# Feed-forward norm weights applied to the turned rows, and a local output projection in four steps

## The reference

```python
x = x + o @ wo                       # local output projection
h = shift_token(x)
mu = h.mean(-1, keepdims=True)
var = h.var(-1, keepdims=True)
h = (h - mu) / jnp.sqrt(var + 1e-05) * lg + lb
h = h @ w1 + b1
a, g = jnp.split(h, 2, axis=-1)
h = a * jax.nn.gelu(g, approximate=False)
x = x + h @ w2 + b2
```

## Time and profile before

| what | value |
|---|---|
| median of 3 runs | 1886.77 us (1885.72 to 1888.03) |
| the profiled execution: its own time | 1886.66 us |
| its span on the core | 1885.10 us |
| time outside the span | 1.56 us |
| TensorE busy share of the span | 93% |
| mean granted TensorE clock | 0.949 of full speed |

### The profile page before, as it was taken

How to read it: one execution, slowest core, us unless ns; L and a number is a source line. 1 busy time by engine, 2 the same in 40 slices (tenths; PEclk the granted TensorE clock), 3 DMA queues, 4 the chain that set the end, 5 groups by cost and what they waited for, 6 DMA issues and landing times. The chain is left out here.

```text
span 1885.1 us, 42756 instructions
## 1 busy us (share of the span) xinstructions
PE 1759.3 (93%) x14072; PEld 1335.8 (71%) x14072; DVE 1144.2 (61%) x2863; ACT 982.9 (52%) x1897; POOL 864.0 (46%) x886
## 2 busy tenths in 40 slices
PE   5899999999779999999988999699999999989997
PEld 3566656666357777777777888577777777768886
DVE  5567766677566766766633433777666776435554
ACT  2556566565545655555553444455565655444443
POOL 3333333333426665555633333555555665235544
PEclk7899888998889999999989999899999999999999
DMA  4433343333010101010023222101100000212221
GB/s 142 143 123 98 123 130 116 123 115 108 26 56 2 33 33 33 33 33 22 11 69 101 67 66 69 56 12 34 33 33 10 24 33 22 80 56 79 89 88 46
DMA packets 105656, 121.29 MB, mean 64 GB/s; under 512 B 23386, under 2 KB 78340, under 8 KB 105604
## 3 DMA queue, kind: packets, MB, share of 16 engines
q1 hardware_dynamic: 99412, 98.08, 16.7%
q0 software_dynamic: 6192, 22.55, 3.3%
HBM read 82.55 MB, written 37.77 MB: 64 GB/s over the span
## 5 line engine op out<-in xcount | busy, mean ns | idle before, releaser
L485 DVE TENSOR_REDUCE a_negm<-d 128x2 f32<-128x256 f32 (+3 forms) x256 | 201.1, 815 | 122.2 <-PE d L631 120.3
L448 ACT ACTIVATE a_PT<-b 128x384 f32<-128x384 f32 (+1 forms) x384 | 185.0, 524 | 135.6 <-PE b L670 69.7
L901 POOL TENSOR_TENSOR l_t<-l_t,l_t 128x512 f32<-128x512 f32 x128 | 165.4, 1293 | 148.3 <-DVE l_t L1053 147.3
L1071 DVE CUSTOM_DVE_ANT_0 d<-d,window 128x256 f32<-128x256 f32 (+1 forms) x512 | 184.3, 421 | 29.1 <-PE d L1171 29.0
L985 ACT ACTIVATE l_PT<-b 128x512 f32<-128x512 f32 (+1 forms) x256 | 125.4, 542 | 109.8 <-PE b L1213 106.3
L1479 POOL TENSOR_TENSOR m_hid_lo<-m_hid,m_hid_hi 128x512 fp32r<-128x512 f32 x80 | 105.1, 1323 | 154.7 <-ACT m_hid_hi L1537 154.5
L1099 PE MATMUL d<-w,l_xt 128*128 128x512 f32 x384 | 165.9, 432 | 3.2 <-DVE l_t L1053 2.3
L1100 PE MATMUL d<-w,l_xt 128*128 128x512 f32 x384 | 152.4, 397 | 0.0
L1101 PE MATMUL d<-w,l_xt 128*128 128x512 f32 x384 | 151.7, 395 | 0.0
L1205 PE MATMUL b<-l_Q,l_K 64*128 64x256 f32 x1536 | 140.3, 295 | 3.2 <-ACT l_PT L985 3.2
L919 POOL TENSOR_TENSOR l_zl<-l_zt,l_zh 128x512 fp32r<-128x512 f32 x64 | 85.7, 1348 | 120.4 <-ACT l_zh L991 120.4
(11 more groups left out here) (228 smaller groups left out, 4915.3 us busy)
## 6 DMA issues: line engine op xcount, KB each, us to landing
a_Q<-qk_parts SPq DMA_DIRECT2D x192, 64.0 KB, 2.1
a_K<-qk_parts SPq DMA_DIRECT2D x192, 64.0 KB, 2.1
qk_parts<-a_qk_hi SPq DMA_DIRECT2D x32, 256.0 KB, 2.1
qk_parts<-a_qk_lo SPq DMA_DIRECT2D x32, 256.0 KB, 2.1
xin<-after_attn SPq DMA_DIRECT2D x32, 256.0 KB, 3.0
m_xr<-after_attn SPq DMA_DIRECT2D x16, 512.0 KB, 3.9
after_attn<-rows_out POOLq DMA_DIRECT2D x14, 512.0 KB, 5.3
xin<-in_L_attn_x SPq DMA_DIRECT2D x8, 512.0 KB, 3.3
```

The costliest lines, as they stand in the source:

```text
L448: nc.scalar.activation(PT[:, p // PG % 2, 2 * (p % PG) + hh, QOFF[t]:QOFF[t] + nq], SC[hh][:, 0:nq], ACT.Exp, scale=AD ** -0.5).then_inc(e ...
L485: dve.tensor_reduce(negm[:, q, 2 * p:2 * p + 2], MX[i % 2][:, :, 0:nk], AX.X, ALU.max, negate=True).then_inc(max_done, 1)
L901: pool.tensor_tensor(t1[:, par, w, :], t1[:, par, w, :], t2[:, par, w, :], ALU.add)\
L1071: m = dve.tensor_tensor_reduce(out=o, in0=o, in1=mask, scale=-1.0, scalar=-NEG, op0=ALU.add, op1=ALU.min, accum_out=negm[:, q + t, p // 2, ...
```

## The change

Four things are different.

The opening of the first stage gets a list of its own (`OPENING`) instead of the filtered list `FIRST` plus `nw:0`. The two lists hold the same steps in the same order.

The local `out` step becomes four steps `out:0` to `out:3`, one for each 128 rows. They stand one behind the other wherever `out:0` stood, so no instruction changes its place. One wait moves: PE's wait on `mrow_done` (ACT's copy of the turned maxima out of the bank that rows 1 and 3 use) stood before all of it and stands now before `out:1`.

The norm weight leaves the split of `w1`: both halves of the tails are now split by one instruction each, and the low parts are plain subtractions. `gam` is loaded with the small vectors.

In `f_te`, ACT now does four instructions instead of two: for each half it reads the turned rows from PSUM twice with `scale=gam` and `bias=bet`, once into `ht_hi` and once into a float32 tile `hf`, which takes the place of `hn` in memory. DVE subtracts `hf` and `ht_hi`, both in SBUF, where it read PSUM before. ACT waits for both halves to be turned, and for the first batch for the small loads. Step `w` is gone, with its wait on `bias_done` ahead of `f_w1`.

```diff
@@ local attention, tensor @@
             elif name == "out":
-                pe.wait_ge(zl_done, b * PAIRS + PAIRS)
-                pe.wait_ge(own.lo_done, KT + 1)
-
-                pe.wait_ge(mrow_done, b * 2 + (2 if isinstance(b, int) else 3))
-                for t in range(TB):
-                    pe.wait_ge(y_done, b * TB + max(t - 1, 0))
...
+                if i == 0:
+                    pe.wait_ge(zl_done, b * PAIRS + PAIRS)
+                    pe.wait_ge(own.lo_done, KT + 1)
+                elif i == 1:
+                    pe.wait_ge(mrow_done, b * 2 + (2 if isinstance(b, int) else 3))
+                pe.wait_ge(y_done, b * TB + max(i - 1, 0))
...
@@ feed-forward weights @@
-            act.wait_ge(self.w_loaded, 32)
-            copy(self.w_hi[:, n, :], self.w_raw[:, n, :], ACT.Copy, scale=gam[:, n:n + 1]).then_inc(self.hi_done, 1)
+            act.wait_ge(self.w_loaded, 16)
+            copy(self.w_hi[:, n, :], self.w_raw[:, n, :], ACT.Copy).then_inc(self.hi_done, 1)
...
-            dve.scalar_tensor_tensor(out=self.w_lo[:, n, :], in0=self.w_raw[:, n, :], scalar=gam[:, n:n + 1],
-                                     in1=self.w_hi[:, n, :], op0=ALU.mult, op1=ALU.subtract).then_inc(self.lo_done, 1)
+            dve.tensor_tensor(self.w_lo[:, n, :], self.w_raw[:, n, :], self.w_hi[:, n, :], ALU.subtract)\
+                .then_inc(self.lo_done, 1)
@@ feed-forward, scalar @@
             if name == "f_m":
                 act.wait_ge(rstd_done, 4 * b + 4)
                 if not isinstance(b, int):
-                    act.wait_ge(turned, b * KT)
+                    act.wait_ge(lo_done, b * KT)
...
             elif name == "f_te":
+                if isinstance(b, int):
+                    act.wait_ge(own.loaded, 96)
+                else:
+                    act.wait_ge(w1_done, b * NT)
+                act.wait_ge(turned, b * KT + KT)
                 for k in range(KT):
-                    act.wait_ge(turned, b * KT + k + 1)
-                    if k == 0 and not isinstance(b, int):
-                        act.wait_ge(w1_done, b * NT)
-                    nc.scalar.activation(ht_hi[:, k, :], FB[k][:, :], ACT.Identity).then_inc(hi_done, 1)
+                    nc.scalar.activation(ht_hi[:, k, :], FB[k][:, :], ACT.Identity, scale=gam[:, k:k + 1],
+                                         bias=bet[:, k:k + 1])
+                    nc.scalar.activation(hf[:, k, :], FB[k][:, :], ACT.Identity, scale=gam[:, k:k + 1],
+                                         bias=bet[:, k:k + 1]).then_inc(scaled, 1)
@@ feed-forward, vector @@
-            if name == "w":
-                dve.wait_ge(bias_full, lay + 1)
...
             elif name == "f_te":
                 for k in range(KT):
-                    dve.wait_ge(hi_done, b * KT + k + 1)
-                    dve.tensor_tensor(ht_lo[:, k, :], FB[k][:, :], ht_hi[:, k, :], ALU.subtract)\
+                    dve.wait_ge(scaled, b * KT + k + 1)
+                    dve.tensor_tensor(ht_lo[:, k, :], hf[:, k, :], ht_hi[:, k, :], ALU.subtract)\
@@ feed-forward, tensor @@
-            elif name == "w":
-                pe.wait_ge(*before.maxima)
-                pe.wait_ge(own.mix_set, 2)
-                pe.wait_ge(own.loaded, 80)
-                for c in range(2 * NF + 1):
...
                 if name == "f_w1" and isinstance(b, int):
-                    if i == 0:
-                        pe.wait_ge(bias_done, 2 * lay + 2)
-                    else:
-                        pe.wait_ge(*before.scores)
+                    pe.wait_ge(*(before.maxima if i == 0 else before.scores))
@@ the joins from local attention to feed-forward @@
-        +f_te:0 pv:1 st:5 ps:2 sv:1 z:1 nm:0 +w:0 st:6 zn:1 zs:0 ns:0 pv:2 sv:2 zs:1 z:2 st:7 zn:2 pv:3 ps:3 +set:0 sv:3
-        zs:2 ns:1 z:3 zn:3 zs:3 +f_w1:0 +f_w1:1 ns:2 out:0 +f_h:0 +f_h:1 +banks:0 +nw:0"""),
+        +f_te:0 pv:1 st:5 ps:2 sv:1 z:1 nm:0 st:6 zn:1 zs:0 ns:0 pv:2 sv:2 zs:1 z:2 st:7 zn:2 pv:3 ps:3 +set:0 sv:3
+        zs:2 ns:1 z:3 zn:3 zs:3 +f_w1:0 +f_w1:1 ns:2 out:0 out:1 out:2 out:3 +f_h:0 +f_h:1 +banks:0 +nw:0"""),
```

More of the change, by code:

```diff
@@ L874, in do @@
                 ahead.load_h(sp, 0)
-            elif name == "out" and isinstance(b, int):
+            elif name == "out" and i == TB - 1 and isinstance(b, int):
                 sp.wait_ge(y_done, end * TB)
@@ L919, in do @@
                 pool.tensor_tensor(zl[:, i, :], zt[:, i, :], zh[:, i, :], ALU.subtract).then_inc(zl_done, 1)
-            elif name == "out" and not isinstance(b, int):
+            elif name == "out" and i == TB - 1 and not isinstance(b, int):
                 pool.wait_ge(y_done, b * TB + TB)
@@ L1336, in high @@
     def high(self, act, n):
-        copy, gam = self.nc.scalar.activation, self.gam
+        copy = self.nc.scalar.activation
         if n < KT:
-            act.wait_ge(self.w_loaded, 32)
-            copy(self.w_hi[:, n, :], self.w_raw[:, n, :], ACT.Copy, scale=gam[:, n:n + 1]).then_inc(self.hi_done, 1)
+            act.wait_ge(self.w_loaded, 16)
+            copy(self.w_hi[:, n, :], self.w_raw[:, n, :], ACT.Copy).then_inc(self.hi_done, 1)
         else:
             act.wait_ge(self.mix_set, 2)
-            for k in range(KT):
-                copy(self.mix_hi[:, k, :], self.mix_raw[:, k, :], ACT.Copy, scale=gam[:, k:k + 1])\
-                    .then_inc(self.hi_done, 1)
+            copy(self.mix_hi[:, :, :], self.mix_raw[:, :, :], ACT.Copy).then_inc(self.hi_done, 1)
             act.wait_ge(self.w2_loaded, 64)
@@ L1379, in feed_forward @@
     NF, TAIL, AT, MIX, NT = own.NF, own.TAIL, own.AT, own.MIX, own.NT
-    w_raw, mix_raw, b1, bet, h, h_in = own.w_raw, own.mix_raw, own.b1, own.bet, own.h, own.h_in
+    b1, gam, bet, h, h_in = own.b1, own.gam, own.bet, own.h, own.h_in
     w_hi, w_lo, mix_hi, mix_lo, w2_hi, w2_lo = own.w_hi, own.w_lo, own.mix_hi, own.mix_lo, own.w2_hi, own.w2_lo
@@ L1429, in do @@
             elif name == "banks":
-                sp.wait_ge(own.lo_done, 2 * KT + 2)
-                sp.wait_ge(bias_full, lay + 1)
+                sp.wait_ge(own.lo_done, KT + 3)
             elif name == "xr":
@@ L1548, in do @@
         def do(name, i, b):
[L1549 to L1560 removed]
+            if name == "f_n":
                 dve.wait_ge(h_in, (b - base) * 32 + 32)
@@ L1576, in do @@
                 n, rows = b * NT + i, P if i < NF else TAIL
+                if name == "f_w1" and isinstance(b, int):
+                    dve.wait_ge(own.loaded, 96)
                 dve.wait_ge(gate_done, n + 1)
@@ L1638, in do @@
                 pe.wait_ge(*before.sums)
-            elif name == "w":
-                pe.wait_ge(*before.maxima)
-                pe.wait_ge(own.mix_set, 2)
-                pe.wait_ge(own.loaded, 80)
-                for c in range(2 * NF + 1):
-                    for f in range(KT):
-                        if c < 2 * NF:
-                            at = HID * (c // NF) + P * (c % NF)
-                            lhs, rows = w_raw[:, f, at:at + P], P
-                        else:
-                            lhs, rows = mix_raw[:, f, :], MIX
-                        m = pe.matmul(AB[0][0][0:rows, c:c + 1], lhs, bet[:, f:f + 1], start=(f == 0),
-                                      stop=(f == KT - 1))
-                m.then_inc(bias_full, 1)
             elif name == "f_t":
@@ L1665, in do @@
                 if i == NF:
-                    pe.wait_ge(own.lo_done, 2 * KT)
+                    pe.wait_ge(own.lo_done, KT + 1)
                 elif i == 0:
@@ L1690, in do @@
                 if i == 0:
-                    pe.wait_ge(own.lo_done, 2 * KT + 2)
+                    pe.wait_ge(own.lo_done, KT + 3)
                     pe.wait_ge(y_done, b * TB)
@@ L1715, in tensor @@
         return do
-    left = Left(front=(lo_done, end * KT), maxima=(hid_done, end * NT - 1), scores=(hid_done, end * NT),
+    left = Left(front=(scaled, end * KT), maxima=(hid_done, end * NT - 1), scores=(hid_done, end * NT),
                 sums=(y_done, end * TB), queries=(w1_done, end * NT), values=(w1_done, end * NT),
@@ L1759 @@
         nx:0 nz:0 xr:0 nw:0 st:0 sm:4 +f_n:0 st:1 ps:0 sm:5 st:2 sm:6 pv:0 +f_m:0 sm:7 sv:0 z:0 st:3 ps:1 zn:0 mt:1 +f_t:0 st:4
-        +f_te:0 pv:1 st:5 ps:2 sv:1 z:1 nm:0 +w:0 st:6 zn:1 zs:0 ns:0 pv:2 sv:2 zs:1 z:2 st:7 zn:2 pv:3 ps:3 +set:0 sv:3
-        zs:2 ns:1 z:3 zn:3 zs:3 +f_w1:0 +f_w1:1 ns:2 out:0 +f_h:0 +f_h:1 +banks:0"""),
+        +f_te:0 pv:1 st:5 ps:2 sv:1 z:1 nm:0 st:6 zn:1 zs:0 ns:0 pv:2 sv:2 zs:1 z:2 st:7 zn:2 pv:3 ps:3 +set:0 sv:3
+        zs:2 ns:1 z:3 zn:3 zs:3 +f_w1:0 +f_w1:1 ns:2 out:0 out:1 out:2 out:3 +f_h:0 +f_h:1 +banks:0"""),
     parse("""w1:2 h:2 w2:0 w1:3 w2:1 w1:4 h:3 h:4 xr:0 w1:5 w2:2 h:5 w2:3 w2:4 w2:5 y:0 fin:0"""),
```

74 lines of the change are left out of this document (31 added, 43 removed).

## The result

The changed kernel took 1861.28 us (median of four runs, 1856.63 to 1865.30) against 1886.24 us for the kernel before in the same session. The ratio is 0.9869, with a 95% interval of 0.9845 to 0.9894. The forecast was 1862.0 us.

What follows compares the result with a forecast made beforehand. PE's own work bounds the loops; in the joins PE's one-column products stand uncovered. Savings of 12.3 and 12.5 us, together 24.8, from 1886.66 gave 1861.9, said as 1862 us; 8-in-10 range 1855 to 1870 us.

Steps and rivals of the forecast that it cites:

- Step `w` gone: Both joins: PE's stop and one-column products, covered by no other engine, go; saves 10.98 us and 11.17 us.
- Rival four (no effect): Joins: something equally long covers PE's 11 us, `f_w1:0` comes no earlier; time within 0.2% of before; chance 3%.
- The rest of the join at full clock: Each join, `st:6` to `f_w1:0`, 12.44 us before in the first: 1.7 us shorter without the low clock.
- `f_te` on ACT: Each join: four ACT instructions instead of two delay the exponentials of `st:5`, costing 0.4 us; bounds 0.1 and 0.8.
- The split of `w1`: Ahead of `f_w1`: same elements on the same engines, so 0; PE's 0.52 us wait bounds any gain.
- The four `out` steps: Local output projection: same instructions and order, only one wait moves; 0, bounds 0 and minus 1.6 us.
- The 14 loop rounds: Feed-forward: longer `f_te` hidden behind PE's `w2` work, 0; cover 0.9 us in layer 0, 0.4 us in layer 1.
- The small loads: ACT's new wait ahead of `f_te`: loads arrive in time, 0; rival of late loads 1870 us, chance 5%.
- The clock behind the join: Behind the join: one low-clock stretch of some 7 us fewer or more moves PE 3.5 us; 1858 to 1866 us.

Runs made afterwards that it cites:

- e1: The kernel before without step `w`, its share of the biases left out, norm weight still in `w1`, `f_te` still two instructions: 1862.71 us, ratio 0.9866.
- e2: The changed kernel with the 22 one-column products put back in their old place on PE, results unused: 1887.61 us, ratio 0.9999 to the kernel before.
- e3: The changed kernel with ten 512-column products on PE in the old place of the 22 one-column ones, results unused: 1884.56 us, ratio 0.9996.
- e4: The changed kernel with PE's wait on `mrow_done` back ahead of row 0 of the output projection: 1864.28 us, ratio 0.9875 to the kernel before.
- e8: The changed kernel itself, unaltered, run once more on another chip: 1862.88 us, ratio 0.9870 to the kernel before.

## Why the prediction was right

**Step `w` gone, 10.98 and 11.17 us.** It was right that nothing covers it. e1 alone gives the whole gain; with e2 and e3 it is gone again. Rival four (no effect) is out.

**The rest of the join at full clock, -1.7 us each.** It came to -2.04: 975.76 - 965.36 = 10.40 us instead of 12.44. The first part is as forecast, 966.91 - 965.36 = 1.55 us from scores to exponentials, against 2.62. The last is unchanged, 4.44 against 4.43. The one between them, between the two groups of exponentials, took 4.41 us, against 5.39, and this was under-sized: -0.98 instead of -0.6. e1, with the clock at 1.00, the old `f_te` and the old split of `w1`, shows how much is the clock: 972.29 - 967.63 = 4.66, so -0.73. The other 0.25 us come from `f_te`, not from the split. In both kernels the exponentials of `st:7` stand behind PE, and from PE's products with values to them it is the same time, 971.32 - 967.28 = 4.04 us in after and 972.29 - 968.27 = 4.02 in e1. What differs is when those products begin: 0.37 us behind the exponentials of `st:6` in after, 0.64 in e1. They wait for the division on DVE (`l_zt`) and begin 0.10 us behind its end in both (966.49 + 0.69 and 967.48 + 0.69), and DVE waits for `l_rr` on ACT. In after PE had finished the sums for `l_rr` while ACT was still in `f_te`, so ACT did not wait for them; in e1 it did, 0.16 us. In the second join the rest took 10.38 us, against 12.25: -1.87.

**`f_te` on ACT, +0.4 us each.** Ahead of `st:6` it cost 0.6: the exponentials of `st:5` came 964.40 - 961.75 = 2.65 us behind its start, where they had come 2.02 us behind. The row with a bias alone gave too low a price: an ACT instruction with scale and offset took 0.79 us, and the next began 0.66 us after it, not 0.69 and 0.6. Of the 0.6 us some 0.25 came back behind it, as just said; the net is the 0.43 us between e1 and after. The under-sized -0.6 and this +0.4 nearly cancel in 12.41 us a join, against 12.3 and 12.5.

**The split of `w1`, 0.** The plain subtraction took 1.65 us in the row above, 1.64 before. ACT's copy took 1.32 to 1.34 us, against 1.43 with `gam` as scale, and PE's wait ahead of `f_w1:0` went from 0.52 to 0.35 us, but from the exponentials of `st:7` to `f_w1:0` it stayed at 4.44 us (4.43 in before and in e1), so none of it was gained.

**The four `out` steps, 0.** So it came out, by e4.

**The 14 loop rounds, 0.** In layer 0 the two covers were there, and in layer 1 DVE was still held by POOL, as in the earlier trace rows. From the timeline of after, a round of each layer:

```profile
1016.14 0.69 DVE L1562 TENSOR_TENSOR m_ht<-m_hf,m_ht 128x512 fp32r<-128x512 f32 x1 [0.79 <-ACT m_hf L1517]
...
1017.52 0.39 PE L1623 MATMUL d<-m_ht,w 128*128 128x512 f32 x1
...
1701.23 2.40 POOL L1481 TENSOR_TENSOR m_xr<-m_xr,m_res 128x1024 f32<-128x1024 f32 x1
...
1701.94 2.23 DVE L1583 TENSOR_TENSOR m_hid_hi<-m_hid,m_hid_hi 42x512 fp32r<-42x512 f32 x1 [0.70 <-ACT m_hid_hi L1537]
...
1704.20 1.29 DVE L1562 TENSOR_TENSOR m_ht<-m_hf,m_ht 128x512 fp32r<-128x512 f32 x2
...
1705.27 0.40 PE L1623 MATMUL d<-m_ht,w 128*128 128x512 f32 x1
```

In layer 0 the first low part is ready at 1016.14 + 0.69 = 1016.83, 0.7 us ahead of PE (cover forecast: 0.9). In layer 1 it is ready near 1704.9, 0.4 us ahead (forecast: 0.4). The subtraction of two SBUF tiles took 0.69 us with POOL idle, as in the earlier trace rows; the 42x512 one took 2.23 us again beside POOL's addition, and ended 1704.17 - 1703.63 = 0.54 us after it. The Trainium skill's rule in SBUF — State Buffer, "Who interferes with whom", that a DVE instruction with two SBUF inputs contends with a GpSimd instruction that reads SBUF, agrees with these rows. As forecast it did not reach `f_te`, because POOL was through.

**The small loads, 0.** Their issue ran until 957.49 + 1.67 = 959.16 here, later than the 953.10 of the earlier trace rows relative to the join (2.6 us ahead of `f_te` instead of 3.2). ACT still went from the exponentials of `st:4` (960.78) to `f_te` (961.75) without idling.

**The clock behind the join, ±3.5 us.** It came out even in the first layer. The low stretch near 1010, 6.8 us, is gone, and two of about 3.4 us each stand at 988 and 1005 in its place. In the second layer before has 3.4 us of low clock near 1676, after none and e8 6.8 us near 1650; so what is seen of this term is scatter between executions, and no run shows the change moving it.

**What would have shown it wrong.** One of my tests fired and meant nothing: ACT starts `f_te` at 961.75, later than 956.4. That test took the time from the start of the span, and so took in the scatter of the first attention; `f_w1:0` at 970.4 fails for the same reason (975.76), while 14.01 us from `f_te` to `f_w1:0` stands beside the 14.07 that the forecast implied. The other tests came out as forecast: no `mw_bet` product, a gap of 0.61 us ahead of `st:6`, clock 1.00, no wait on `m_ht`.

**What was luck.** That the median came within 0.7 us of 1862 is more than the forecast could promise: the four runs lie between 1856.63 and 1865.30 us. What bears it out are the joins, 12.41 us each, and there two errors of opposite sign helped: the rest of the join at -2.04 instead of -1.7 us, `f_te` at 0.6 instead of 0.4.

## What to carry to other kernels

Look for stretches in which one engine works and the others' busy time is zero: what stood there counted in full here, even though its results were tiny, and it could be priced from two rows. Once such a piece is gone, read the join again for the next engine whose order holds it up (here DVE's split of `w2` ahead of a row that PE waits for, 2.9 us a join), and before an ACT step is moved ask which exponentials it will then stand in front of. Give a test of a forecast as a length between two landmarks of the same stage, never as a time from the start of the program.
